# An elementwise product of a selective-scan stage, moved from VectorE to GpSimd

## Chip, core and metric

One core of one Trainium2 chip. The metric is the device time of one launch in microseconds. The traced execution is shown with it; its span runs from the first to the last instruction of the trace.

## What is computed

The kernel is one block: adaptive layer norm, a mamba layer, a residual, another adaptive layer norm, and a mixture of experts with a residual. Input x is 4 x 2048 x 256 in float32. The change touches the mamba layer alone, of which this matters:

```python
xs = silu(causal_conv(x @ in_proj_w[:512].T) + conv_b)       # b, l, 512
dt, B, C = split(xs @ x_proj_w.T, [64, 80])
delta = softplus(dt @ dt_proj_w.T + dt_proj_b)               # b, l, 512
A = -exp(A_log)                                              # 512, 16
h[t] = exp(delta[t] * A) * h[t-1] + (delta[t] * xs[t]) * B[t]  # 512 x 16 states
y[t] = sum over the 16 states of h[t] * C[t]
out = (y * silu(res)) @ out_proj_w.T
```

The factor `delta * xs` (one value for each channel and time step, shared by the 16 states) is the product that the change moves.

## The kernel before

Four programs run one behind the other: setup, mamba, the shared expert with the routing, and the routed experts. The mamba program goes through 16 chunks of 512 time steps, four to a sequence. Within a chunk there are 16 sets s = 0 to 15 of 32 channels each; a set has 32 channels x 16 states, held as 128 partitions x 4 groups x 512 steps in a ring of eight tiles `hs`. Bodies for chunks 0, 1, 14 and 15 are written out; chunks 2 to 13 run in a loop of four.

For each set the work goes round the engines:

- `states_in` (L620 on VectorE, L709 on GpSimd) multiplies u = delta * xs, replicated over the states, by B and writes `hs`. For ten sets ("own": 0, 1, 3, 4, 6, 8, 9, 11, 12, 14) VectorE does this from `u_ps`, which TensorE's `spread_u` (L427) fills by a matmul with a 0/1 matrix. For the six "shared" sets (2, 5, 7, 10, 13, 15) GpSimd does it from `u_rep`, which four DMAs of SP's queue (L335) fill. Both read `us[:, half]`, and both wait for `du_ready`.
- ScalarE makes `dA` = exp(delta * A) (L555), four of a set, three ahead of the scans at most.
- VectorE scans (`scan_set`, L641), four scans of 128x512 for a set. ScalarE saves the last column as the state (`save`, L560).
- GpSimd multiplies the scanned set by C (`weigh_states`, L724).
- TensorE sums over the states (`sum_states`, L437), four sets at a time, at steps s = 1, 5, 9, 13; it needs `weigh_states` of these four sets. Its result `y_ready` lets the ring tiles be filled again: `states_in` of sets 4, 8 and 12 on VectorE, and of each shared set on GpSimd, wait for it. VectorE gates y with silu(res) (`gate_y`, L654).

Besides, each engine prepares the next chunks at fixed steps of the present one. TensorE's order is the table `plan`: XS (input projection, L396), CV (convolution, L400), RS, XP (L404), DT and DB (L407), T (transposes of the normalized x, L391), OP (output projection, L415). They share two PSUM banks, so each waits for the eviction of the last but one. At s = 14 TensorE does, in this order, T 0, T 1 (for chunk c + 2) and `spread_u` of set 0 (chunk c + 1); at s = 15 XS 0, XS 1 (chunk c + 2) and `spread_u` of set 1. ScalarE evicts what `evict` names, runs `normalize` (L536) at s = 14, and silu, exp and log at the steps of L244. `delta` for the next chunk is finished by VectorE's `add_delta` (L617) after the scans of sets 11 and 12, and `weigh_u` (L648) then makes `us = delta * us` for all 512 channels in one instruction of 128x2048, after the scan of set 13. It releases `du_ready`.

GpSimd's order in a chunk: weigh_states s for s = 0 to 15, the product of set 5 after s = 1, 7 after 3, 10 after 5, 13 after 8, 15 after 10, and that of set 2 of the next chunk after 14. After s = 11 it runs `rsqrt` (L700 to L707), four small instructions on 128x4 for the layer norm of chunk c + 2.

SP's queue carries all transfers of this stage in order. At the end of a chunk: `spread_bc` (B and C of the next chunk), `spread_delta` of quarter 0 (d_rep, L326), `spread_u` of set 2 (L335), and then the next chunk's d_rep of quarter 1, u_rep of sets 5 and 7, and the residual's input. `hold` is a wait for a semaphore with an increment of another behind it.

Of the kernel before, what the change touches and what calls it, by code (L numbers as in the profile page):

```python
# [21 lines left out]
ALU = mybir.AluOpType  # L22
# [13 lines left out]
KI = DI // P  # L36
# [20 lines left out]
def hold(eng, sem, value, held):  # L57


    eng.wait_ge(sem, value)  # L60
    eng.sem_inc(held, 1)  # L61
# [132 lines left out]
def mamba_program(nc, ins, t, bc_dram, x1_dram, wout_dram):  # L194
# [4 lines left out]
    with ExitStack() as ctx:  # L199
# [7 lines left out]
        xpad, us, res = t["xpad"], sb("us", [P, 2, KI, T]), sb("res", [P, 2, KI, T])  # L207
        xdbl = sb("xdbl", [PROJ, T])
        delta, xres = sb("delta", [P, KI, T]), sb("xres", [P, TT, D])
# [10 lines left out]
        xdbl_made, dt_made, db_made, out_made = sem("xdbl_made"), sem("dt_made"), sem("db_made"), sem("out_made")  # L220
        halo_ready = sem("halo_ready")
        xs_ready, us_pre, us_ready, res_pre, res_ready = sem("xs_ready"), sem("us_pre"), sem("us_ready"), sem("res_pre"), sem("res_ready")
        xdbl_ready, bc_kept, bc_loaded = sem("xdbl_ready"), sem("bc_kept"), sem("bc_loaded")
        abs_ready, exp_ready, log_ready, delta_ready, du_ready = sem("abs_ready"), sem("exp_ready"), sem("log_ready"), sem("delta_ready"), sem("du_ready")
# [4 lines left out]
        held, wout_loaded = sem("held"), sem("wout_loaded")  # L229
# [11 lines left out]
                 10: [("RS", 3)], 15: [("T", 0), ("T", 1)]}  # L241
        SHARED_AT = {1: (5,), 3: (7,), 5: (10,), 8: (13,), 10: (15,), 14: (2,)}
        RESIDUAL_AT, DELTA_AT = {4: (0,), 5: (1,)}, {11: (0, 1), 12: (2, 3)}
        SUM_AT, SILU_AT, SILU_RES_AT, EXP_AT, LOG_AT, STATS_AT, RSTD_AT, DU_AT, NORM_AT, EARLY = 1, 5, 11, 9, 10, 11, 11, 13, 14, 14  # L244
        order = [g for s in range(NSET) for g in plan.get(s, [])]
        back = [g for g in order if g[0] == "OP"]
        early = [g for s in range(EARLY, NSET) for g in plan.get(s, []) if g not in back]
# [8 lines left out]
        has_front = lambda c: not (known(c) and c == NCHUNK - 1)  # L256
# [27 lines left out]
        def read_bank(eng, g, f):  # L284
            eng.wait_ge(made[g[0]], many[g[0]] * f + g[1] + 1)
            return banks[bank_of[g]]
# [311 lines left out]
        @block.vector  # L598
        def _(dve):
            def layernorm(f):  # L600
                dve.wait_ge(x_loaded, 16 * f + 16)
                for tt in range(TT):
                    last = nc.vector.bn_stats(stats[:, tt, :], xin[:, tt, :])
                last.then_inc(ln_step, 1)
                hold(dve, ln_step, f + 1, held)
                if not (known(f) and f == 0):
                    hold(dve, xn_ready, f, held)
                for tt in range(TT):
                    last = nc.vector.bn_aggr(mv[:, tt, :], stats[:, tt, :])
                last.then_inc(stats_ready, 1)  # L610

            def add_delta(f, j):

                ps_ = read_bank(dve, ("DB", j), f)
                if j == 0:
                    dve.wait_ge(log_ready, f + 1)
                nc.vector.scalar_tensor_tensor(out=delta[:, j, :], in0=ps_[:, :], scalar=0.0, in1=delta[:, j, :],  # L617
                                               op0=ALU.max, op1=ALU.add).then_inc(delta_ready, 1)

            def states_in(c, s, par):  # L620

                i = OWN_SETS.index(s)
                dve.wait_ge(u_made, N_OWN * c + i + 1)
                if s % KI == 0 and not (known(c) and c == 0 and s < RING):
                    dve.wait_ge(y_ready, SPC * c + (s - RING) // KI + 1)
                if s == 0:
                    dve.wait_ge(bc_loaded, 16 * 2 * NF * (c + 1))
                nc.vector.tensor_tensor(hs[:, s % RING], u_ps[:, i % 2, :].unsqueeze(1).to_broadcast([P, NG, T]),  # L628
                                        b_rep[:, par, :].rearrange("p (g t) -> p g t", g=NG), ALU.mult).then_inc(dbu_own, 1)

            def scan_set(c, s, m):
                if s in OWN_SETS:
                    dve.wait_ge(dbu_own, N_OWN * c + OWN_SETS.index(s) + 1)
                else:
                    dve.wait_ge(dbu_shared, N_SHARED * c + SHARED_SETS.index(s) + 1)
                if m:
                    dve.wait_ge(state_saved, NSET * (c - 1) + s + 1)
                for g in range(NG):
                    u = NG * s + g
                    dve.wait_ge(da_ready, NG * NSET * c + u + 1)  # L640
                    nc.vector.tensor_tensor_scan(hs[:, s % RING, g, :], dA[:, u % ABANK, :], hs[:, s % RING, g, :], state[:, u:u + 1] if m else 0.0,  # L641
                                                 ALU.mult, ALU.add).then_inc(scan_done, 1)

            def weigh_u(f, half):
                dve.wait_ge(delta_ready, KI * (f + 1))
                dve.wait_ge(us_ready, f + 1)
                dve.wait_ge(xdbl_made, f + 1)
                nc.vector.tensor_tensor(us[:, half], delta[:], us[:, half], ALU.mult).then_inc(du_ready, 1)  # L648

            def gate_y(c, j, half):  # L650
                dve.wait_ge(y_ready, KI * c + j + 1)
                if j == 0:
                    dve.wait_ge(res_ready, c + 1)
                nc.vector.tensor_tensor(res[:, half, j, :], y_ps[:], res[:, half, j, :], ALU.mult).then_inc(yg_ready, 1)  # L654

            def residual(c, j):

                ps_ = read_bank(dve, ("OP", j), c - 1)
                if j == 0:
                    dve.wait_ge(xres_loaded, 16 * c)  # L660
                nc.vector.tensor_tensor(xres[:, 2 * j:2 * j + 2, :], ps_[:].rearrange("p (h d) -> p h d", h=2), xres[:, 2 * j:2 * j + 2, :],
                                        ALU.add).then_inc(x1_ready, 1)

            def body(c, m):
                par = m % 2
                states_in(c, 0, par)
                for s in range(NSET):
                    if s + 1 in OWN_SETS and (s + 1) % KI:
                        states_in(c, s + 1, par)
                    scan_set(c, s, m)  # L670
                    if s + 1 in OWN_SETS and (s + 1) % KI == 0:
                        states_in(c, s + 1, par)
                    if has_ahead(c) and s == STATS_AT:
                        layernorm(c + 2)
                    if has_back(c) and s == 3:
                        gate_y(c - 1, SPC - 1, 1 - par)
                    if has_back(c):
                        for j in RESIDUAL_AT.get(s, ()):
                            residual(c, j)
                    if s > SPC and s % SPC == 3:  # L680
                        gate_y(c, s // SPC - 1, par)
                    if has_front(c):
                        for j in DELTA_AT.get(s, ()):
                            add_delta(c + 1, j)
                        if s == DU_AT:
                            weigh_u(c + 1, 1 - par)

            layernorm(0)
            for j in range(KI):
                add_delta(0, j)  # L690
            weigh_u(0, 0)
            layernorm(1)
            bodies(dve, body)
            gate_y(NCHUNK - 1, KI - 1, 1)
            residual(NCHUNK, 0)
            residual(NCHUNK, 1)

        @block.gpsimd
        def _(pool):
            def rsqrt(f):  # L700
                hold(pool, stats_ready, f + 1, held)
                nc.gpsimd.tensor_scalar(var[:], mv[:, :, 1], EPS, None, ALU.add).then_inc(rstd_step, 1)
                nc.gpsimd.tensor_scalar(mean[:], mv[:, :, 0], -1.0, None, ALU.mult).then_inc(rstd_step, 1)
                hold(pool, rstd_step, 3 * f + 2, held)
                nc.gpsimd.tensor_tensor(rstd[:], var[:], t["mhalf"][:, 0:TT], ALU.pow).then_inc(rstd_step, 1)
                hold(pool, rstd_step, 3 * f + 3, held)
                nc.gpsimd.tensor_tensor(shift[:], mean[:], rstd[:], ALU.mult).then_inc(shift_ready, 1)  # L707

            def states_in(c, s, par):  # L709

# [16 lines left out]
            def body(c, m):  # L727
                par = m % 2
                for s in range(NSET):
                    weigh_states(c, s, par)  # L730
                    for n in SHARED_AT.get(s, ()):
                        if n > s:
                            states_in(c, n, par)
                        elif has_front(c):
                            states_in(c + 1, n, 1 - par)
                    if s == RSTD_AT and has_ahead(c):
                        rsqrt(c + 2)

            rsqrt(0)
            rsqrt(1)  # L740
            for s in range(NSET):
                for n in SHARED_AT.get(s, ()):
# [611 lines left out]
```

## Time and profile before

| what | us |
|---|---|
| median of 3 runs | 3006.31 (3005.31 to 5768.12) |
| profiled execution | 3006.31 |
| its span | 3004.6 |

```profile
PE 2258.5 (75%) x7448; PEld 1050.1 (35%) x7449; DVE 2068.5 (69%) x2313; ACT 1320.5 (44%) x2151; POOL 1936.9 (64%) x800
PE   4678687688687787687787784349988930999998
DVE  3299999999999999999989999824444440222222
ACT  1465565565665665665665664302222200222221
POOL 0189889889989889889889889900000016455553
PEclk7778688687787787787787786679999975999999
```

PE is TensorE, DVE VectorE, ACT ScalarE, POOL GpSimd. The first line gives busy time, its share of the span and the number of instructions. The others cut the span in 40 slices of 75 us, with the busy share in tenths; PEclk is TensorE's granted clock in tenths of 2.4 GHz. The mamba stage is slices 3 to 26, where VectorE is at 9 and GpSimd at 8 or 9.

### The profile page before, as it was taken

How to read it: one execution, taken by the hardware profiler on the slowest of the kernel's cores; microseconds unless marked ns; L12 is line 12 of the kernel's file. 1: busy time of each engine (PE TensorE's matmuls, PEld its weight loads, DVE VectorE, ACT ScalarE, POOL GpSimd, SP SyncE). 2: the span in 40 equal slices, each digit the busy share in tenths (PEclk: the TensorE clock that was granted, in tenths of full speed). 3: DMA queues.
4: the chain of work that ended last, by engine and by line, in shares of the span. 5: the costliest groups of instructions: out<-in, count | busy, mean ns of one | idle time of the engine just before them, and what ended most of it. 6: DMA issues, size and time to landing. Idle time of an engine off the chain costs nothing. (4 is left out here: it accounts for less than half of the span.)

```text
span 3004.6 us, 29127 instructions
## 1 busy us (share of the span) xinstructions
PE 2258.5 (75%) x7448; PEld 1050.1 (35%) x7449; DVE 2068.5 (69%) x2313; ACT 1320.5 (44%) x2151; POOL 1936.9 (64%) x800
## 2 busy tenths in 40 slices
PE   4678687688687787687787784349988930999998
PEld 3223233233233233232232231135555520556654
DVE  3299999999999999999989999824444440222222
ACT  1465565565665665665665664302222200222221
POOL 0189889889989889889889889900000016455553
PEclk7778688687787787787787786679999975999999
DMA  3333433433433433424424342152111100222221
GB/s 110 75 75 74 99 82 74 99 84 78 102 75 72 102 79 80 102 65 90 94 75 93 90 94 63 35 217 63 63 50 55 63 23 7 84 84 85 86 85 51
DMA packets 113435, 238.40 MB, mean 79 GB/s; under 512 B 21516, under 2 KB 75534, under 8 KB 100752
## 3 DMA queue, kind: packets, MB, share of 16 engines
q1 hardware_dynamic: 93328, 189.86, 25.9%
q0 software_dynamic: 14368, 36.00, 4.1%
q10 hardware_dynamic: 5600, 11.01, 1.0%
q8 instruction: 48, 0.79, 0.1%
q14 instruction: 91, 0.75, 0.1%
HBM read 106.10 MB, written 39.20 MB: 48 GB/s over the span
## 5 line engine op out<-in xcount | busy, mean ns | idle before, releaser
L724 POOL TENSOR_TENSOR hs<-hs,c_rep 128x2048 f32<-128x2048 f32 x256 | 1158.3, 4540 | 80.0 <-ACT state L560 79.8
L555 ACT ACTIVATE dA<-d_rep,a 128x512 f32<-128x512 f32 x1024 | 683.6, 686 | 603.7 <-DVE hs L641 599.5
L641 DVE TENSOR_TENSOR_SCAN hs<-dA,state,hs 128x512 f32<-128x512 f32 x768 | 915.3, 1259 | 27.1 <-ACT dA L555 25.9
L717 POOL TENSOR_TENSOR hs<-u_rep,b_rep 128x2048 f32<-128x2048 f32 x96 | 433.4, 4514 | 106.0 <-PE y_ps L437 98.3
L396 PE MATMUL bank<-xin,w_in 128*128 128x512 f32 x512 | 333.2, 805 | 110.4 <-ACT xpad L491 86.3
L628 DVE TENSOR_TENSOR hs<-u_ps,b_rep 128x2048 f32<-128x2048 f32 x160 | 363.9, 2275 | 73.6 <-PE u_ps L427 72.8
L437 PE MATMUL y_ps<-hs,gather 128*32 128x512 f32 x2048 | 279.7, 695 | 134.1 <-POOL hs L724 134.1
L407 PE MATMUL bank<-xdbl,w_dt 65*128 65x512 f32 x256 | 181.3, 846 | 172.4 <-DVE delta L617 115.3
L641 DVE TENSOR_TENSOR_SCAN hs<-dA,hs 128x512 f32<-128x512 f32 x256 | 290.0, 1199 | 12.1 <-ACT dA L555 12.0
L822 POOL TENSOR_TENSOR rstd<-var,mhalf 128x4 f32<-128x4 f32 x16 | 16.1, 1006 | 409.4 <-DVE var L924 409.4
L1204 PE MATMUL z<-w1r,hT 128*128 x560 | 261.0, 609 | 2.6 <-issue 1.9
L1286 DVE TENSOR_TENSOR hid<-z,sg 128x512 f32<-128x512 f32 x70 | 48.4, 691 | 298.6 <-ACT sg L1264 298.6
L400 PE MATMUL bank<-xpad,w_conv 128*128 128x512 f32 x512 | 234.9, 607 | 4.1 <-ACT us L501 4.1
L396 PEld LDWEIGHTS bank<-xin,w_in 128*128 128x128 f32 x512 | 126.6, 258 | 305.9 <-issue 161.1
L427 PE MATMUL u_ps<-us,spread 32*128 32x512 f32 x320 | 212.7, 750 | 21.8 <-DVE hs L628 20.8
L437 PEld LDWEIGHTS y_ps<-hs,gather 128*32 128x32 f32 x2048 | 67.3, 126 | 359.9 <-issue 208.4
L1171 POOL DMA_INDIRECT out<-outr,cur x70 | 71.1, 1016 | 142.9 <-DVE outr L1279 142.6
L407 PEld LDWEIGHTS bank<-xdbl,w_dt 65*128 65x128 f32 x256 | 58.2, 252 | 270.2 <-DVE delta L617 136.5
L1204 PEld LDWEIGHTS z<-w1r,hT 128*128 128x128 f32 x560 | 101.6, 191 | 120.5 <-issue 120.4
L400 PEld LDWEIGHTS bank<-xpad,w_conv 128*128 128x128 f32 x512 | 94.1, 191 | 141.6 <-issue 124.5
L868 PE MATMUL y_ps<-w2s,hid 128*128 128x256 f32 x512 | 119.1, 386 | 20.5 <-DVE yg L975 18.1
L1222 PE MATMUL y_ps<-w2r,hidT 128*128 x560 | 132.4, 379 | 0.8 <-ACT hidT L1253 0.8
(169 smaller groups left out, 2640.3 us busy)
## 6 DMA issues: line engine op xcount, KB each, us to landing
d_rep<-delta SPq DMA_DIRECT2D x256, 256.0 KB, 4.3
u_rep<-us SPq DMA_DIRECT2D x384, 64.0 KB, 2.2
b_rep<-bc_rows SPq DMA_DIRECT2D x64, 256.0 KB, 4.5
c_rep<-bc_rows SPq DMA_DIRECT2D x64, 256.0 KB, 7.4
xin<-in_x SPq DMA_DIRECT2D x16, 512.0 KB, 3.7
xres<-in_x SPq DMA_DIRECT2D x16, 512.0 KB, 3.6
x<-xres SPq DMA_DIRECT2D x16, 512.0 KB, 4.5
x_sb<-x SPq DMA_DIRECT2D x16, 512.0 KB, 4.2
```

What stands on the lines that cost most here:

```text
L396: last = nc.tensor.matmul(ps_[:, :], t["w_in"][:, k, col:col + P], hT[:, k, :], start=(k == 0), stop=(k == KD - 1))
L400: last = nc.tensor.matmul(ps_[:, :], t["w_conv"][:, j, k, :], xpad[:, j, k:k + T], start=(k == 0), stop=(k == KCONV - 1))
L407: last = nc.tensor.matmul(ps_[:, :], t["w_dt"][:, j * P:(j + 1) * P], xdbl[0:DT_ROWS, :], start=True, stop=True)
L427: nc.tensor.matmul(u_ps[:, i % 2, :], t["spread"][DS * q:DS * q + DS].rearrange("p f d -> p (f d)"), us[DS * q:DS * q + DS, par, j, :], st ...
L437: last = nc.tensor.matmul(y_ps[DS * q:DS * q + DS, :], t["gather"][:], hs[:, (SPC * j + q) % RING, g, :], start=(g == 0), stop=(g == NG - ...
L555: nc.scalar.activation(dA[:, u % ABANK, :], d_rep[:, q % 2, j, :], ACT.Exp, scale=t["a"][:, u:u + 1]).then_inc(da_ready, 1)
L628: nc.vector.tensor_tensor(hs[:, s % RING], u_ps[:, i % 2, :].unsqueeze(1).to_broadcast([P, NG, T]), b_rep[:, par, :].rearrange("p (g t) -> ...
L641: nc.vector.tensor_tensor_scan(hs[:, s % RING, g, :], dA[:, u % ABANK, :], hs[:, s % RING, g, :], state[:, u:u + 1] if m else 0.0, ALU.mul ...
L717: nc.gpsimd.tensor_tensor(hs[:, s % RING], u_rep[:, i % UBUF, :].unsqueeze(1).to_broadcast([P, NG, T]), b_rep[:, par, :].rearrange("p (g t ...
L724: nc.gpsimd.tensor_tensor(hs[:, s % RING, :, :], hs[:, s % RING, :, :], c_rep[:, par, :].rearrange("p (g t) -> p g t", g=NG), ALU.mult).th ...
L1204: last = nc.tensor.matmul(z[:, q % 2, half, :], hT[:, q % 2, i, :], t["w1r"][:, e, i, half * H:(half + 1) * H], start=(i == 0), stop=(i == ...
L1222: last = nc.tensor.matmul(y_ps[:, :], hidT[:, q % 2, i, :], t["w2r"][:, e, i, :], start=(i == 0), stop=(i == KI - 1))
```

## The change

`weigh_u` moves from VectorE's program to GpSimd's, as the same product on the same tiles. On VectorE it stood after the scan of set 13 (DU_AT = 13). On GpSimd it stands after `weigh_states` of set 12 (DU_AT = 12), behind `rsqrt` of set 11. The first one, for chunk 0, stands between `rsqrt(0)` and `rsqrt(1)`. Its three waits stay; the one for `delta_ready` is now a `hold`, since another engine makes it.

```diff
-        SUM_AT, SILU_AT, SILU_RES_AT, EXP_AT, LOG_AT, STATS_AT, RSTD_AT, DU_AT, NORM_AT, EARLY = 1, 5, 11, 9, 10, 11, 11, 13, 14, 14
+        SUM_AT, SILU_AT, SILU_RES_AT, EXP_AT, LOG_AT, STATS_AT, RSTD_AT, DU_AT, NORM_AT, EARLY = 1, 5, 11, 9, 10, 11, 11, 12, 14, 14
@@ VectorE
-            def weigh_u(f, half):
-                dve.wait_ge(delta_ready, KI * (f + 1))
-                dve.wait_ge(us_ready, f + 1)
-                dve.wait_ge(xdbl_made, f + 1)
-                nc.vector.tensor_tensor(us[:, half], delta[:], us[:, half], ALU.mult).then_inc(du_ready, 1)
-
@@ VectorE, body
-                        if s == DU_AT:
-                            weigh_u(c + 1, 1 - par)
@@ VectorE, before the bodies
-            weigh_u(0, 0)
@@ GpSimd
+            def weigh_u(f, half):
+                hold(pool, delta_ready, KI * (f + 1), held)
+                pool.wait_ge(us_ready, f + 1)
+                pool.wait_ge(xdbl_made, f + 1)
+                nc.gpsimd.tensor_tensor(us[:, half], delta[:], us[:, half], ALU.mult).then_inc(du_ready, 1)
@@ GpSimd, body
+                    if s == DU_AT and has_front(c):
+                        weigh_u(c + 1, 1 - par)
 
             rsqrt(0)
+            weigh_u(0, 0)
             rsqrt(1)
```

## Rows read from the trace of the kernel before

**Rows 1.** Busy time by stretch: us, then busy and count for each engine, clock, DMA.
```profile
0.00:1968.00 1968.00, 1433.80 (x4496) 554.60 (x4497) 1738.57 (x1560) 1115.78 (x1795) 1636.68 (x432) 0.78 0.35 83
```

**Rows 2.** VectorE's groups, 200 to 1900 us: busy us, mean ns, idle before.
```profile
L641 DVE TENSOR_TENSOR_SCAN hs<-dA,state,hs 128x512 f32<-128x512 f32 x737 | 878.5, 1259 | 27.1 <-ACT dA L555 25.9
...
L648 DVE TENSOR_TENSOR us<-delta,us 128x2048 f32<-128x2048 f32 x15 | 38.0, 2533 | 0.0
```

**Rows 3.** GpSimd's largest group, 200 to 1900 us.
```profile
L724 POOL TENSOR_TENSOR hs<-hs,c_rep 128x2048 f32<-128x2048 f32 x241 | 1090.9, 4541 | 63.8 <-ACT state L560 63.6
```

**Rows 4.** Waits, 200 to 1900 us: who waited for whom, total, times, longest.
```profile
POOL 0189889889989889889889889900000016455553
...
DVE hs L628 <- PE u_ps L427: 55.7, 29, 3.6
```

**Rows 5.** GpSimd's timeline in chunk 7: start, duration, instruction, idle before.
```profile
1007.66 4.51 POOL L717 TENSOR_TENSOR hs<-u_rep,b_rep 128x2048 f32<-128x2048 f32 x1 [5.40 <-PE y_ps L437]
...
1032.08 2.34 POOL L707 TENSOR_TENSOR shift<-mean,rstd 128x4 f32<-128x4 f32 x1 [0.18 <-POOL rstd L705]
1034.38 13.48 POOL L724 TENSOR_TENSOR hs<-hs,c_rep 128x2048 f32<-128x2048 f32 x3
...
1057.88 4.51 POOL L724 TENSOR_TENSOR hs<-hs,c_rep 128x2048 f32<-128x2048 f32 x1 [1.09 <-ACT state L560]
```

**Rows 6.** VectorE's timeline in chunk 7 and at the start of chunk 8.
```profile
1032.10 2.26 DVE L648 TENSOR_TENSOR us<-delta,us 128x2048 f32<-128x2048 f32 x1
...
1044.28 2.28 DVE L628 TENSOR_TENSOR hs<-u_ps,b_rep 128x2048 f32<-128x2048 f32 x1
1050.08 2.29 DVE L628 TENSOR_TENSOR hs<-u_ps,b_rep 128x2048 f32<-128x2048 f32 x1 [3.52 <-PE u_ps L427]
```

**Rows 7.** TensorE's timeline there; each matmul leaves two records.
```profile
1030.11 5.84 PE L437 MATMUL y_ps<-hs,gather 128*32 128x512 f32 x32 [5.50 <-POOL hs L724]
1038.33 1.97 PE L391 MATMUL bank<-ident,xin 128*128 128x128 f32 x8 [2.37 <-ACT xin L536]
1040.23 2.07 PE L427 MATMUL u_ps<-us,spread 32*128 32x512 f32 x2
1042.40 6.60 PE L396 MATMUL bank<-xin,w_in 128*128 128x512 f32 x8
1048.92 1.12 PE L427 MATMUL u_ps<-us,spread 32*128 32x512 f32 x2
```

**Rows 8.** GpSimd's timeline in chunks 0 and 14, and its end of chunk 15.
```profile
211.72 4.52 POOL L717 TENSOR_TENSOR hs<-u_rep,b_rep 128x2048 f32<-128x2048 f32 x1 [6.14 <-PE y_ps L437]
...
238.28 0.20 POOL L707 TENSOR_TENSOR shift<-mean,rstd 128x4 f32<-128x4 f32 x1 [0.18 <-POOL rstd L705]
...
1803.35 4.51 POOL L717 TENSOR_TENSOR hs<-u_rep,b_rep 128x2048 f32<-128x2048 f32 x1 [5.06 <-PE y_ps L437]
...
1927.39 22.39 POOL L724 TENSOR_TENSOR hs<-hs,c_rep 128x2048 f32<-128x2048 f32 x5
```

**Rows 9.** VectorE's timeline, `weigh_u` in chunk 14.
```profile
1826.07 6.32 DVE L648 TENSOR_TENSOR us<-delta,us 128x2048 f32<-128x2048 f32 x1
```

**Rows 10.** TensorE's timeline, XS 0 and 1 in chunks 0 and 13.
```profile
244.73 5.37 PE L396 MATMUL bank<-xin,w_in 128*128 128x512 f32 x8 [1.88 <-ACT xin L488]
...
1724.74 5.06 PE L396 MATMUL bank<-xin,w_in 128*128 128x512 f32 x8
```

**Rows 11.** VectorE's timeline, the product of set 1 after chunks 0 and 13.
```profile
251.18 2.29 DVE L628 TENSOR_TENSOR hs<-u_ps,b_rep 128x2048 f32<-128x2048 f32 x1 [2.57 <-PE u_ps L427]
...
1730.89 2.29 DVE L628 TENSOR_TENSOR hs<-u_ps,b_rep 128x2048 f32<-128x2048 f32 x1 [1.99 <-PE u_ps L427]
```

**Rows 12.** The page's DMA issues: KB each, median us from issue to landing.
```profile
u_rep<-us SPq DMA_DIRECT2D x384, 64.0 KB, 2.2
```

**Rows 13.** TensorE's timeline in the prologue.
```profile
70.36 3.70 PE L396 MATMUL bank<-xin,w_in 128*128 128x512 f32 x8 [0.69 <-ACT xpad L491]
```

**Rows 14.** TensorE by stretch, chunk 7: us, busy (records), granted clock, DMA.
```profile
1042.00:1044.00 2.00, 1.90 (x3) 0.50 0.95 197
```

## The prediction

> **What bounds the kernel now.** I read the page's busy shares and slices first, then the busy time by stretch, then the groups of each engine, the waits, and at last the timelines of one chunk on three engines. The reader should see four things.
>
> First, the change lies wholly in the first 1968 us, the mamba stage, where VectorE is busy 1738.6 us and GpSimd 1636.7 us [rows 1]. Two engines are near full, so work taken from one lands on another that has little room.
>
> Second, VectorE's work there is mostly the scans at 1.26 us each; the instruction to be moved is one of 128x2048 per chunk, 38.0 us for 15 of them in that window [rows 2]. 15 of the 16 lasted 2.26 us, one 6.32. GpSimd's main instruction has the same form (two SBUF inputs, 128x2048, f32) and takes 4.54 us [rows 3]: this is the price on GpSimd.
>
> Third, neither engine is simply full. VectorE loses 55.7 us in 29 waits for u_ps from TensorE, GpSimd 98.3 us in 29 waits for y_ps [rows 4]. So each chunk is a loop through several engines, and the loop's path decides, not a sum of busy time.
>
> Fourth, where the loop runs. I take chunk 7 and three points. S is the start of GpSimd's `states_in` for set 13, which waited 5.40 us for TensorE: 1007.66. From S GpSimd works without a gap through weigh_states 9, 10, the product of set 15, weigh_states 11, the four small instructions of `rsqrt`, and weigh_states 12, which starts at 1034.38 [rows 5]. On VectorE `weigh_u` ran at 1032.10; the first product of the next chunk, set 0, began at 1044.28, and that of set 1 at 1050.08, after 3.52 us of waiting for TensorE [rows 6]; call this last point R. On TensorE the order is: sum_states, two transposes T, `spread_u` of set 0 (1040.23), XS 0 and 1 (1042.40), `spread_u` of set 1 (1048.92) [rows 7]. XS began as soon as ScalarE had evicted T, which lies behind VectorE's scan of set 15. So R minus S went through VectorE: 42.42 us in this chunk.
>
> **What the change does, step by step.**
>
> *Taken from VectorE.* One `weigh_u` a chunk, 2.26 us, 2.2 from its start to the next. All VectorE points behind it come 2.2 us earlier, if nothing else holds them.
>
> *Taken from GpSimd.* A gain that the diff does not name. `rsqrt`'s last instruction took 2.34 us in chunk 7 and ended just as `weigh_u` did [rows 5, 6]; in chunk 0 the same instruction took 0.20 us [rows 8], and the hold fell on another instruction. In each of chunks 0 to 13 one GpSimd instruction is 1.2 to 2.1 us too long while `weigh_u` runs. In chunk 14, where `rsqrt` is left out, `weigh_u` met a large GpSimd instruction and lasted 6.32 us, 4.06 more than usual [rows 9]. So the two engines shut each other out in this form. The other VectorE instructions there read at most one SBUF tensor beside PSUM and run over GpSimd's without such a trace. I take 2.1 us as the relief.
>
> The Trainium skill says the same ("SBUF — State Buffer", Who interferes with whom): a VectorE instruction with two SBUF inputs contends with a GpSimd one that reads SBUF, and the first to start holds the port throughout. By that rule the product on GpSimd, beside PSUM-fed VectorE work, stalls nobody; without the relief each chunk's end below would come 2.1 us later. The trace agrees with the rule: 0.20 against 2.34 us.
>
> *Added to GpSimd.* One `weigh_u`, 4.51 us, after weigh_states 12. Its end D, counted from S: weigh_states 12 starts at 26.72 (1034.38 - 1007.66), less 2.14 of relief = 24.58, plus 4.49 for it and 4.51 for the new product, D = S + 33.6. Its own waits cost nothing: `add_delta` 3 stands before `weigh_u` on VectorE today, which began at 1032.10 [rows 6], and the product on GpSimd starts at S + 29.1 = 1036.8. Today `us` is ready at 1034.3, S + 26.6. So it is ready 7 us later, though VectorE is 2.2 us earlier.
>
> *Who is queued behind.* TensorE waits in order: `spread_u` of set 0 needs `du_ready`, and XS 0, XS 1 and `spread_u` of set 1 stand behind it. Today XS starts at S + 34.02 on average (14 chunks, first 33.01, last 34.51 [rows 8, 10]). After, `spread_u` of set 0 starts at D + 0.1 = S + 33.7. It takes 1.12 us in 10 of the 14 chunks and 2.07 in 4, mean 1.39; XS 0 and 1 take 5.06 to 6.69, mean 5.74 (14 rows, first 5.37, last 5.06 [rows 10]); `spread_u` of set 1 takes 1.12 [rows 7]. With overlaps of 0.07 at the two joins: 33.7 + 1.32 + 5.67 + 1.16 to VectorE's start = S + 41.9. Today R is at S + 40.85 on average (14 chunks; first 251.18 - 211.72 = 39.46 [rows 8, 11]). So R comes 1.0 us later: 14 x 1.0 = +14 us. The 2.2 us of VectorE are gone, as a longer wait for u_ps.
>
> *From R to the next S.* 72.8 us in the mean, and I take it as unchanged, since it is made by VectorE, ScalarE and TensorE in turns. The 14 differences lie close together (last 1803.35 - 1730.89 = 72.5 [rows 8, 11]; longest 73.5). For that GpSimd must not be late at the next set 13. It starts the next chunk's weigh_states 0 at D + 18 = S + 51.6, where today it is at S + 50.2 [rows 5]. It is 1 to 3 us late, and then has its 1.09 us of waits for ScalarE and the 5.40 at set 13 to catch up [rows 5]. The sum agrees: 22 large instructions at 4.48, `rsqrt` 2.2 and the product 4.5 make 105.3 us, against a period of 113.7 (1803.35 - 211.72 over 14 [rows 8]).
>
> *SP's queue.* The u_rep transfers of set 2 wait for `du_ready` too, and the next d_rep behind them. Between D and its use GpSimd has weigh_states 13 and 14, 9 us; from issue to landing such a transfer takes 2.2 us [rows 12], and four are issued in 2.4: hidden. Without that work between, it would cost about 4.6 us.
>
> *Chunk 14 and the end.* Nothing is transposed there, and VectorE wins 6.2 us. But in the second half of the last chunk GpSimd runs without a pause: weigh_states 11 to 15 go in one piece and end at 1949.8 (1927.39 + 22.39 [rows 8]), with TensorE's last sum behind them. Up to there its queue also got 4.5 us more. I give 2 us of the 6 as gain. The prologue's product is 2.3 us longer once; XS of chunk 1 stands before `spread_u` there, so I count zero (cover gone: +2.3).
>
> **Sum.** 14 x 1.0 - 2 = +12 us. The profiled execution is itself the median run, 3006.3 (span 3004.6). Forecast 3018.7 us.
>
> **Bounds of the unknown term.** It is TensorE's pace over twelve matmul records right behind a wait. All fast: XS in 3.70 as in the prologue [rows 13], R at S + 39.5, 1.3 earlier: 14 x -1.3 - 2 = -20, 2986 us. All at the lower level, as in chunk 7 (granted clock 0.50 of 2.4 GHz, so 1.2 [rows 14]): 2.07, 6.60 and 2.07 give S + 44.3, 3.5 later: +47, 3053 us. I take the mean of the 14 because the clock there falls and rises within most chunks. A wait of 3 to 4 us in front pushes to the slow side, so I keep it near the middle, not below.
>
> **Rivals.**
> 1. *VectorE's gain survives.* If `us` is early enough on GpSimd, or TensorE's order does not pin XS, each chunk wins 2.2 us: 14 x -2.2 - 2 = -33, 2973 us. For it: VectorE is the busiest engine. Against: D is at S + 33.6, and twelve records do not fit between it and S + 38.6, even at the fast pace (5.8 us).
> 2. *Slower, by TensorE's clock.* TensorE now stands idle from the end of T to S + 33.7; T ended at S + 32.6 in chunk 7 (1038.33 + 1.97 [rows 7]) and comes up to 2.2 us earlier with VectorE. If the clock is then low for all that follows, and also in the stretch from R to S (73.5 us in the slowest chunk against 72.8), each chunk loses 3.5 + 0.7: 14 x 4.2 - 2 = +57, 3063 us. It decides if more than about ten of the twelve records run at 1.2 GHz. For it: chunk 7 is such a one. Against: 9 of the 14 XS pairs took under 5.5 us.
> 3. *GpSimd itself becomes the bound.* Needs 113.7 us of work, has 105.3: it would need 8 us more a chunk. Only then would time rise by more than 2%.
> 4. *Nothing moves*: later u_ps exactly eats the early VectorE, 3006 us within 5. It is inside the forecast's own range.
>
> **Chances.** Forecast mechanism (GpSimd's product sets XS), 2986 to 3045: 0.72, rival 4 in it. Rival 1: 0.14. Rival 2: 0.10. Rival 3: 0.02; others 0.02. For 8 in 10 the range runs from 2975, the end of rival 1, to 3050. By more than 2% (60 us, about what a measurement here can tell from no change) faster: 0.02, since even rival 1 gives 1.1%. Slower by more than 2%: half of rival 2 and rival 3, 0.07. Within 2%: 0.91.
>
> **What would show it.** No VectorE instruction of 128x2048 from two SBUF tensors; 16 of 4.5 us on GpSimd; `rsqrt`'s four never longer than 1.04. VectorE's waits for u_ps grow from 55.7 to over 85 us, those of GpSimd for y_ps shrink from 98 to about 60. TensorE waits for GpSimd's `us` 3 us in each chunk, before `spread_u` of set 0. XS starts at S + 35. It would be wrong if R minus S fell below 40, if GpSimd stopped waiting at set 13, or if R to S changed by more than 1 us.

## The result

| | median us | runs |
|---|---|---|
| before | 3003.34 | 20 |
| changed | 3036.19 | 20 |

The ratio is 1.0104, 95% interval 1.0091 to 1.0117: the change costs 1.04%, some 33 us. The traces say 3035.2 against 3004.6 us of span. Among the 20 executions of the kernel before, one took 5768 us and one 3036; the median isn't moved by them.

The table compares the two traces by the points that the prediction used (S: GpSimd's product of set 13; R: VectorE's product of set 1; means over chunks 0 to 13, worked out from the timelines).

| us from S | before | forecast | changed |
|---|---|---|---|
| product on GpSimd ends (D) | - | 33.6 | 33.6 |
| `spread_u` of set 0 starts | 31.3 | 33.7 | 33.7 |
| its duration | 1.39 | 1.39 | 1.96 |
| XS 0 and 1, duration | 5.74 | 5.74 | 6.04 |
| R | 40.85 | 41.9 | 42.76 |
| from R to the next S | 72.84 | 72.8 | 73.10 |

The waits, 200 to 1900 us: first the engine and line that waited, then who was waited for, the total, the times and the longest. The first line of [rows 4] is one of the page's slices and no wait; the wait of the kernel before that the prediction reads as 98.3 us is this one:

```profile
POOL hs L717 <- PE y_ps L437: 98.3, 29, 6.3
```

The changed kernel:

```profile
DVE hs L628 <- PE u_ps L427: 115.8, 46, 4.9
...
POOL hs L714 <- PE y_ps L437: 96.4, 29, 6.1
...
PE u_ps L427 <- POOL us L704: 62.0, 15, 4.3
```

VectorE's wait for u_ps doubled, from 55.7 us, and TensorE has a new wait of 62.0 us in 15 times for GpSimd's `us`. That is the queue that the prediction described. Chunk 7 on GpSimd, the answer to [rows 5]:

```profile
1020.83 4.51 POOL L714 TENSOR_TENSOR hs<-u_rep,b_rep 128x2048 f32<-128x2048 f32 x1 [5.34 <-PE y_ps L437]
...
1045.23 0.20 POOL L698 TENSOR_TENSOR shift<-mean,rstd 128x4 f32<-128x4 f32 x1 [0.18 <-POOL rstd L696]
1045.42 4.55 POOL L721 TENSOR_TENSOR hs<-hs,c_rep 128x2048 f32<-128x2048 f32 x1
1049.94 4.50 POOL L704 TENSOR_TENSOR us<-delta,us 128x2048 f32<-128x2048 f32 x1
```

The product ends at 1054.44, S + 33.61. The last instruction of `rsqrt` takes 0.20 us, where it took 2.34. TensorE and VectorE in the same chunk, to be held against [rows 7] and [rows 6]:

```profile
1043.26 5.80 PE L437 MATMUL y_ps<-hs,gather 128*32 128x512 f32 x32 [5.63 <-POOL hs L721]
1049.15 1.09 PE L391 MATMUL bank<-ident,xin 128*128 128x128 f32 x8
1054.57 2.07 PE L427 MATMUL u_ps<-us,spread 32*128 32x512 f32 x2 [4.33 <-POOL us L704]
1056.56 6.05 PE L396 MATMUL bank<-xin,w_in 128*128 128x512 f32 x8
1062.54 1.12 PE L427 MATMUL u_ps<-us,spread 32*128 32x512 f32 x2
```

```profile
1040.40 14.20 DVE L641 TENSOR_TENSOR_SCAN hs<-dA,state,hs 128x512 f32<-128x512 f32 x12
1054.51 0.67 DVE L648 TENSOR_TENSOR res<-y_ps,res 128x512 f32<-128x512 f32 x1
1056.85 2.29 DVE L628 TENSOR_TENSOR hs<-u_ps,b_rep 128x2048 f32<-128x2048 f32 x1 [1.67 <-PE u_ps L427]
1063.70 2.29 DVE L628 TENSOR_TENSOR hs<-u_ps,b_rep 128x2048 f32<-128x2048 f32 x1 [4.56 <-PE u_ps L427]
```

VectorE runs its twelve scans of sets 13 to 15 without the product in between and then waits twice, 1.67 and 4.56 us, for TensorE. TensorE stands idle for 4.33 us after the transposes, and the two records of `spread_u` behind that wait take 2.07 us, XS 6.05.

### The profile page after: what moved, and what is told of

The parts are those of the page before. It is cut to its first block and busy times, and to the rows that moved or that the text cites. A ratio compares the mean times of both kernels' runs of the same rounds, so it can differ in the third digit from the quotient of the medians.

```text
span 3035.2 us, 29143 instructions
## 1 busy us (share of the span) xinstructions
PE 2270.4 (75%) x7448; PEld 1053.1 (35%) x7449; DVE 2030.8 (67%) x2297; ACT 1321.1 (44%) x2151; POOL 1980.8 (65%) x816
## 5 line engine op out<-in xcount | busy, mean ns | idle before, releaser
L396 PE MATMUL bank<-xin,w_in 128*128 128x512 f32 x512 | 342.9, 826 | 91.2 <-ACT xpad L491 86.3
L427 PE MATMUL u_ps<-us,spread 32*128 32x512 f32 x320 | 222.2, 782 | 72.8 <-POOL us L704 62.0
L1286 DVE TENSOR_TENSOR hid<-z,sg 128x512 f32<-128x512 f32 x70 | 48.4, 692 | 298.4 <-ACT sg L1264 298.4
```

What stands on the lines that cost most here:

```text
L396: last = nc.tensor.matmul(ps_[:, :], t["w_in"][:, k, col:col + P], hT[:, k, :], start=(k == 0), stop=(k == KD - 1))
L427: nc.tensor.matmul(u_ps[:, i % 2, :], t["spread"][DS * q:DS * q + DS].rearrange("p f d -> p (f d)"), us[DS * q:DS * q + DS, par, j, :], st ...
```

## The experiments

Three theories were held against each other. **Queue**: time is lost because `us` comes late to TensorE, with XS and the second `spread_u` behind it. **Load**: the 4.5 us more on GpSimd (or what VectorE does) set the pace. **Clock**: a large part is TensorE's pace behind the idle time. All times are medians, and the ratios are against the kernel before, which took 3005 to 3006 us beside each of these runs. Where a run is compared with the changed kernel, that is the 3036.19 us above. "XS" stands for XS 0 and 1 together, eight records.

### The product one place earlier on GpSimd

```diff
- ... RSTD_AT, DU_AT, NORM_AT, EARLY = ... 11, 12, 14, 14
+ ... RSTD_AT, DU_AT, NORM_AT, EARLY = ... 11, 11, 14, 14
```

> The changed kernel with the product on GpSimd one place earlier, after rsqrt of set 11 and before weigh_states 12. Queue theory (the time is lost because `us` reaches TensorE's queue late, with XS 0 and 1 behind it): the product ends at S + 29.1 instead of S + 33.6, before TensorE's transposes end, so XS again starts right behind ScalarE's eviction of T, 2.2 us earlier than in the kernel before; S to R falls from 42.8 to about 38.7 us, and the time to about 3036 - 14 x 4.1 = 2979 us, under that of the kernel before by some 25. Load theory (GpSimd with 4.5 us more a chunk is what costs): nothing changes, 3036 us.

Measured: 2962.9 us, ratio 0.986 (0.9845 to 0.9878). The profiled execution took 2949.8, two of the six runs being near 2950 and four near 2963. The product ends at S + 29.2, and TensorE waits at most 0.26 us for it. Chunk 7, S = 977.55:

```profile
1006.24 1.09 PE L391 MATMUL bank<-ident,xin 128*128 128x128 f32 x8
1007.27 1.12 PE L427 MATMUL u_ps<-us,spread 32*128 32x512 f32 x2
1009.04 3.70 PE L396 MATMUL bank<-xin,w_in 128*128 128x512 f32 x8 [0.65 <-ACT xin L488]
```

The load theory falls: GpSimd has the same work and the time is 73 us less. The median went 16 us below the expected 2979. The trace is of one of the two faster executions, 29 us below it. In this trace XS took 3.67 to 3.70 us in 8 of the 14 chunks and 5.40 in six, which makes the mean S to R 37.4 us against the expected 38.7, 18 us in all. R to S is 0.5 us shorter than in the changed kernel, another 8 us. There is no trace of an execution near 2963, so what sets the two groups apart isn't shown; their granted clock over the whole execution was 0.832 against 0.840. The move to GpSimd as such is good; the place in the order made it bad.

In the eight faster chunks TensorE had stood idle for 0.64 to 1.05 us before XS, in the six others for 1.85 to 1.93, as here in chunk 5:

```profile
783.18 1.12 PE L427 MATMUL u_ps<-us,spread 32*128 32x512 f32 x2
786.23 5.40 PE L396 MATMUL bank<-xin,w_in 128*128 128x512 f32 x8 [1.93 <-ACT xin L488]
```

### XS 0 ahead of `spread_u` on TensorE

```diff
                         if is_there(g, c):
                             group(g, c, chunk_of(g, c), par)
+                        if g == ("XS", 0) and has_front(c):
+                            spread_u(c + 1, 0, 1 - par)
...
-                    if s + 2 >= NSET and has_front(c):
+                    if s + 2 > NSET and has_front(c):
```

> The changed kernel with TensorE's `spread_u` of set 0 moved behind XS 0 (before XS 1); GpSimd as in the changed kernel. Queue theory: XS 0 starts at S + 32 (T evicted), `spread_u` 0 at about S + 35, XS 1 ends at S + 39; S to R about 40 instead of 42.8, TensorE's waits for `us` nearly gone, time about 3036 - 14 x 2.8 = 2997 us. Load theory: 3036 us.

Measured: 2978.0 us, ratio 0.991 (0.9892 to 0.9925). GpSimd is untouched, the product still ends at S + 33.6, and 58 us are gone. Chunk 7, S = 996.20:

```profile
1027.71 1.98 PE L396 MATMUL bank<-xin,w_in 128*128 128x512 f32 x4 [1.70 <-ACT xin L490]
1029.96 1.12 PE L427 MATMUL u_ps<-us,spread 32*128 32x512 f32 x2 [0.26 <-POOL us L706]
1031.00 1.98 PE L396 MATMUL bank<-xin,w_in 128*128 128x512 f32 x4
```

XS 0 fills the wait, which is down to 0.26 us here. VectorE's product of set 0 starts no earlier than before (S + 36.2 in the mean, 35.9 in the changed kernel), and R comes at S + 39.2 instead of 42.8. So it was what stood behind the late `us` that counted, not the lateness of set 0 itself. Again the gain is larger than expected (58 against 39 us), and again the matmuls are at the fast pace here: 1.98 us for an XS group. The swap closes the idle time too, so this run holds queue and clock together and does not share the 58 us out between them; the next one holds the order fixed.

### Matmuls into the idle time

```diff
-                if i == 0:
-                    pe.wait_ge(du_ready, c + 1)
                 if not (known(c) and c == 0 and i < 2):
                     pe.wait_ge(dbu_own, N_OWN * c + i - 1)
+                if i == 0:
+                    if not (known(c) and c == 0):
+                        for _ in range(4):
+                            nc.tensor.matmul(u_ps[:, 0, :], t["ident"][:], t["w_in"][:, 0, 0:T], start=True, stop=True)
+                    pe.wait_ge(du_ready, c + 1)
```

> The changed kernel with four added 128x512 matmuls on TensorE between T 1 and the wait for `us` (their result is overwritten by `spread_u`). They fill the 4.3 us in which TensorE is idle, if they run at the higher clock (3.4 us). Clock theory (0.9 of the 1.9 us of later R come from TensorE being at 1.2 GHz after that idle time): `spread_u` 0 takes 1.1 instead of 2.07 us and XS below 5.5 instead of 6.05, S to R falls by 1.5 us or more, time about 3015 us. If the clock doesn't depend on it, no change or, where the four run at 1.2 GHz (6.8 us), a later XS: 3036 to 3080 us.

Measured: 2987.8 us, ratio 0.994 (0.9926 to 0.9959). TensorE does more, in the same place of the same order, and the kernel is 48 us faster than the changed one, and faster than the kernel before. Chunk 7, S = 994.55:

```profile
1023.84 3.60 PE L428 MATMUL u_ps<-w_in,ident 128*128 128x512 f32 x8
1028.23 1.12 PE L430 MATMUL u_ps<-us,spread 32*128 32x512 f32 x2 [0.79 <-POOL us L707]
1029.28 3.70 PE L396 MATMUL bank<-xin,w_in 128*128 128x512 f32 x8
1032.91 1.12 PE L430 MATMUL u_ps<-us,spread 32*128 32x512 f32 x2
```

The twelve records behind the wait take 5.8 us instead of 9.1. The granted clock over these stretches, first of this kernel (1.00, 2.4 GHz throughout), then of the changed one (0.63, a mix of both levels); columns are those of [rows 14]:

```profile
1028.20:1034.00 5.80, 5.77 (x12) 1.00 0.52 113
```

```profile
1054.50:1063.70 9.20, 9.10 (x12) 0.63 0.68 144
```

S to R is 39.5 us in each chunk, which is the fast bound of the prediction (S + 39.5). The changed kernel has 42.76 in the mean: 3.25 us a chunk, 14 x 3.25 = 45.5 us, and 48.4 were measured.

### Two instead of four

```diff
-                        for _ in range(4):
+                        for _ in range(2):
```

> The changed kernel with two added matmuls in front of the wait for `us` instead of four (four gave 2988 us). They cover 1.7 of the 4.3 us of TensorE's idle time. Clock theory, if what counts is how long TensorE stands idle in front of XS: part of the gain, some chunks with XS at 3.7 us and some with 5.4 to 6, 3000 to 3025 us. If the four only helped by something else than the idle time they fill (their place, or the wait that moved in front of them), two give the same 2988 us.

Measured: 3033.6 us, ratio 1.0095 (1.0078 to 1.0112). Below the expected gain: 13 of 14 chunks kept XS at 5.06 to 6.43 us, and one, chunk 1, had 3.70. Chunk 7:

```profile
1045.80 1.88 PE L428 MATMUL u_ps<-w_in,ident 128*128 128x512 f32 x4
1050.23 2.07 PE L430 MATMUL u_ps<-us,spread 32*128 32x512 f32 x2 [2.55 <-POOL us L707]
1052.23 6.08 PE L396 MATMUL bank<-xin,w_in 128*128 128x512 f32 x8
```

With 2.55 us of idle time left instead of 4.33, nearly all the cost is still there; with 0.79 us left none is. The added matmuls as such, or the wait that moved in front of them, are not what helped. The cost goes by steps, not in proportion to the idle time. Chunk 1, the one at the fast pace, had 2.10 us of idle time left, the others 2.28 to 2.57.

### Other work on VectorE

```diff
+                        if s == 13:
+                            for i in range(6):
+                                nc.vector.bn_stats(pad[:, i, :], t["w_in"][:, 0, 0:D])
```

> The changed kernel with about 2.1 us of other work on VectorE after the scan of set 13, where `weigh_u` stood (six bn_stats of 128x256 of a weight, into an unused tile). Queue theory: VectorE waits 1.7 + 4.6 us for u_ps a chunk in the changed kernel, so this is hidden: 3036 us within 4, and the waits of VectorE for u_ps fall by about 2 us a chunk. If VectorE's load bounds the chunk: +2.1 x 15 = 3067 us.

Measured: 3036.8 us, ratio 1.0104 (1.0088 to 1.0121), as the changed kernel. In chunk 7:

```profile
1045.06 2.04 DVE L681 BATCH_NORM_STATS2 pad<-w_in 128x6 f32<-128x256 f32 x6
...
1057.00 2.28 DVE L628 TENSOR_TENSOR hs<-u_ps,b_rep 128x2048 f32<-128x2048 f32 x1
1063.65 2.29 DVE L628 TENSOR_TENSOR hs<-u_ps,b_rep 128x2048 f32<-128x2048 f32 x1 [4.37 <-PE u_ps L427]
```

The 2.04 us vanish in the wait before set 0, which was 1.67 us, and a little of the next. What the change took from VectorE is therefore worth nothing in the changed kernel. On TensorE the transposes come about 2 us later in ten of the 14 chunks, behind ScalarE's normalize, and so part of its idle time lies in front of them. In chunk 7 that leaves 2.39 us in front of `spread_u` instead of 4.33, and XS took 6.03 us all the same.

### The product one place later on GpSimd

```diff
- ... RSTD_AT, DU_AT, NORM_AT, EARLY = ... 11, 12, 14, 14
+ ... RSTD_AT, DU_AT, NORM_AT, EARLY = ... 11, 13, 14, 14
```

> The changed kernel with the product on GpSimd one place later, behind weigh_states 13. Queue theory: it ends at S + 38.1, everything behind it in TensorE's queue moves by the full 4.5 us, S to R is 47.3 us: 3036 + 14 x 4.5 = 3099 us. Load theory (only GpSimd's work counts, not its place): 3036 us.

Measured: 3087.5 us, ratio 1.0277 (1.026 to 1.0294): 51 us more than the changed kernel, not 63. The product ends at S + 38.1 as worked out, S to R is 46.8 us in the mean, 4.1 more instead of 4.5, since XS took 5.5 instead of 6.04 us, and R to S shrank by 0.4. So lateness is paid almost in full from S + 33.6 to S + 38.1, and this time not through the clock, which moves the price by some tenths the other way. TensorE in chunk 7:

```profile
1085.75 2.06 PE L427 MATMUL u_ps<-us,spread 32*128 32x512 f32 x2 [8.65 <-POOL us L704]
1087.74 5.45 PE L396 MATMUL bank<-xin,w_in 128*128 128x512 f32 x8
```

Behind 8.65 us of idle time XS was 0.6 us faster than behind 4.33: more idle time in front is not always a slower pace. Why is open.

### `weigh_u` on VectorE, one set earlier

The kernel before, with its DU_AT at 12 instead of 13.

> The kernel before with `weigh_u` still on VectorE but one set earlier, behind add_delta 3 (set 12). `us` is ready some 14 us before TensorE asks for it, and XS waits for T as it did. Queue theory: no gain from the earlier `us`, 3005 us within 8. Port theory (the two engines shut each other out for these products): it now meets one of GpSimd's large instructions in each chunk, so that one such instruction a chunk lasts about 6.6 instead of 4.5 us, or `weigh_u` lasts longer than 2.26 us. Without exclusion both keep 4.5 and 2.26.

Measured: 2991.5 us, ratio 0.9955 (0.9938 to 0.9972). That is 14 us under the 3005.6 beside it, which was not expected. GpSimd and VectorE in chunk 7:

```profile
1019.06 6.58 POOL L724 TENSOR_TENSOR hs<-hs,c_rep 128x2048 f32<-128x2048 f32 x1
```

```profile
1018.99 2.29 DVE L648 TENSOR_TENSOR us<-delta,us 128x2048 f32<-128x2048 f32 x1
```

VectorE's product started first and weigh_states 11 lasted 6.58 instead of 4.5 us. This is the exclusion seen in [rows 9] and [rows 5], here with GpSimd's large instruction as the one held. Over the run `weigh_u` took 2.29 to 4.35 us. sum_states starts about 2 us later therefore, XS starts at S + 34.9 instead of 34.0, and yet S to R is 39.8 instead of 40.85 us, since XS took 3.7 us in 13 of 14 chunks:

```profile
1036.21 3.70 PE L396 MATMUL bank<-xin,w_in 128*128 128x512 f32 x8 [1.92 <-ACT xin L488]
```

Behind the same 1.92 us XS took 5.40 to 6.66 us in four chunks of the kernel before, as in chunk 6:

```profile
926.84 6.35 PE L396 MATMUL bank<-xin,w_in 128*128 128x512 f32 x8 [1.92 <-ACT xin L488]
```

So the idle time right in front of XS does not by itself decide its pace. Here the transposes follow sum_states without idle time (at most 0.2 us, but for chunk 0); in the kernel before TensorE stood idle for 0.4 to 2.7 us in front of them. That the clock is higher because the work behind sum_states lies closer together is my reading; this run does not separate it.

### Two matmuls behind `spread_u`

```diff
+                if i == 0 and not (known(c) and c == 0):
+                    pe.wait_ge(dbu_own, N_OWN * c)
+                    for _ in range(2):
+                        nc.tensor.matmul(u_ps[:, 1, :], t["ident"][:], t["w_in"][:, 0, 0:T], start=True, stop=True)
```

In the kernel before:

> The kernel before with two added 128x512 matmuls on TensorE behind `spread_u` of set 0 (into the half of u_ps that set 1 overwrites), where it stood idle for 1.8 to 2 us before XS 0. Clock theory: XS at 2.4 GHz, 3.7 instead of 5.6 us, S to R 39 instead of 40.85 us, 3003 - 14 x 1.8 = 2978 us; a little less if the two delay XS. Otherwise 3003 us or up to 20 more.

Measured: 2984.3 us (2977 to 3000), ratio 0.9939 (0.9915 to 0.9964). XS took 3.7 us in 11 of the 14 chunks and 3.83 to 4.07 in the rest. So the kernel before, too, was paying for the clock, 21 us against the 3005.6 beside it. In chunk 7 of this run `weigh_u` started 0.13 us behind a large product of GpSimd and took 6.54 us:

```profile
1017.26 11.05 POOL L728 TENSOR_TENSOR hs<-hs,c_rep 128x2048 f32<-128x2048 f32 x2
```

```profile
1017.39 6.54 DVE L652 TENSOR_TENSOR us<-delta,us 128x2048 f32<-128x2048 f32 x1
```

S to R was 47.9 us there against 37.6 to 41.2 in the others. In the kernel before, `weigh_u` met GpSimd's small instructions in 13 of the chunks 0 to 13 (in chunk 6 it started just ahead of weigh_states 12, which then took 6.62 us), and this one shows what it can cost when GpSimd's large one starts first.

With the product on GpSimd before weigh_states 12, and the same two matmuls:

> The product on GpSimd before weigh_states 12 (as in the first experiment of this study, 2963 us) with the same two added matmuls behind `spread_u` of set 0. 6 of its 14 chunks had XS at 5.40 us, the rest at 3.70; clock theory: all at 3.7, worth 6 x 1.7 = 10 us; the two added ones take 1.7 us where the gap is 1.0 to 2.0, so XS starts up to 0.7 us later in eight chunks: 2950 to 2962 us. If it is nothing: 2963 us or more.

Measured: 2954.0 us, ratio 0.983 (0.9814 to 0.9847). XS took 3.6 to 3.7 us in all 14 chunks. This is the lowest median of the study, 52 us under the 3005.6 beside it. TensorE in chunk 7:

```profile
1011.76 1.98 PE L432 MATMUL u_ps<-w_in,ident 128*128 128x512 f32 x4
1013.58 3.60 PE L396 MATMUL bank<-xin,w_in 128*128 128x512 f32 x8
```

The expectation took "six chunks at 5.40 us" from the trace of the 2950 us execution and the 2963 us from the median, which do not belong together. Trace against trace, S to R is 37.4 us in both kernels: what XS gains, its later start takes back. The four executions here (2952.7 to 2956.5) lie below the 2963 group of the first experiment and above its two at 2950. So the two matmuls lowered the median by 9 us, and that they did it through XS in the slower group is likely but not shown, since no trace of that group exists.

### Three more in front of sum_states

```diff
+                    if s == 13:
+                        pe.wait_ge(dbu_own, N_OWN * (c + 1) - 1)
+                        for _ in range(3):
+                            nc.tensor.matmul(u_ps[:, 0, :], t["ident"][:], t["w_in"][:, 0, 0:T], start=True, stop=True)
```

> The product before weigh_states 12, the two added matmuls behind `spread_u` of set 0 (2954 us), and three more in front of sum_states at step 13, where TensorE stands idle for 6.8 us and sum_states then takes 6.4 instead of 3.6 us. Clock theory: sum_states at up to 2.4 GHz, T 1 to 2.7 us earlier. What stands behind T is held by ScalarE's normalize and its eviction after the scans of set 15, so little of it comes through: 2945 to 2955 us. If the three run long at 1.2 GHz and hold up sum_states, 2960 us.

Measured: 2968.0 us, ratio 0.9875 (0.9859 to 0.9892), 14 us slower than without them. sum_states of chunk 7 did go at the fast pace, 3.64 us, but S to R and R to S grew by 0.3 and 0.5 us in the mean. The 0.3 us are the two matmuls behind `spread_u`. In seven of the 14 chunks they took 3.2 to 3.7 us instead of 1.98, and R came at about S + 38.5, in the others at S + 36.8. Chunk 2:

```profile
463.25 3.68 PE L432 MATMUL u_ps<-w_in,ident 128*128 128x512 f32 x4
466.76 3.60 PE L396 MATMUL bank<-xin,w_in 128*128 128x512 f32 x8
```

So the filling can itself run at the slow pace and then holds up what stands behind it. Where the 0.5 us from R to S come from is open.

## Why the prediction was right in its mechanism and wrong in its size

**What bounds the kernel: right.** A loop through GpSimd, TensorE and VectorE with S and R on it. Moving the product by one place changed the time by -73 and +51 us, with the engines' instructions unchanged.

**The price on GpSimd and the relief: right.** 4.50 us and D = S + 33.61, with 33.6 forecast. The 0.20 us of `rsqrt`'s last instruction in all chunks, against 0.20 to 2.42 before, bear out that VectorE's product used to hold GpSimd's. (Over the 14 chunks the hold was 1.1 to 2.2 us, 1.8 in the mean. The sum used chunk 7's own 2.14 with chunk 7's own start, so D is not hurt by it.) The Trainium skill's rule ("SBUF — State Buffer", Who interferes with whom) agrees with the trace here: 6.58 us for a GpSimd product when VectorE's two-input one starts first, 6.54 for VectorE's when GpSimd's does.

**Who is queued behind: right.** TensorE waits 4.1 us a chunk for `us` (3 forecast; the transposes end earlier, at S + 29.5 instead of 31.3, as their waits for normalize fell from 22.1 us in all to 1.6). VectorE's 2.2 us are gone.

**The step that failed is the term for TensorE's pace over the twelve records behind the wait.** The prediction gave it the mean of the 14 chunks before, 1.39 and 5.74 us, and named a longer wait's push to the slow side without pricing it. Measured: 1.96 and 6.04 us, 0.87 us more a chunk, 14 x 0.87 = 12 us. The sum has a second and smaller miss, R to the next S, 0.26 us longer, 3.7 us. And the gain at the end was 1.0 us of time to the stage's end (164.7 from S of chunk 14 before, 163.8 after) instead of 2. With the forecast's 12 this makes 29 us; 1.7 of the 30.6 us between the spans lie behind the mamba stage (1038.2 against 1036.5 us), which the change does not touch.

The mean of before was the wrong price because TensorE's idle time lies elsewhere. Before, `spread_u` followed the transposes at once and XS came behind 0.1 to 2.0 us of waiting; now all twelve records stand behind 4.2 us (3.8 to 4.3). The experiments with four and two matmuls show that in the changed kernel filling this time frees the twelve from the low clock, and filling less than half of it does not. They do not give a rule by which the pace could have been foretold: in other kernels of this study XS took 3.7 us in one and 5.4 to 6.7 us in another behind the same 1.92 us, and was faster behind 8.65 than behind 4.33. What else decides is open.

All twelve at 2.4 GHz give S + 39.5 and a kernel of 2988 us, so the clock over these records is worth 48 us in the changed kernel, more than the change's loss of 33. Without it, the change with its queue would have beaten the kernel before as that one ran, though not that kernel with its own XS at the fast pace (2984 us).

**Rivals.** Rival 1 (VectorE's gain survives) was wrong for this change, but its condition, `us` early enough, was met one place earlier, and the kernel then took 2963 us, 10 less than the 2973 of that rival; the surplus is not the rival's doing, since in the trace XS ran at the fast pace in 8 chunks and R came at S + 37.4, where the rival had S + 38.6. Rival 2 (the clock) was the missing part: seven or eight of the twelve records ran slow in chunk 7 (two of `spread_u`, and (6.05 - 3.70) / 0.43 = 5.5 of XS), short of the ten to twelve it wanted, and the time came to lie between forecast and rival. Rival 3 fell: GpSimd still waits 5.5 us at set 13 (5.6 before).

**The sign that was wrong.** GpSimd's waits for y_ps were to shrink from 98 to about 60 us and stayed at 96. The 38 us less are the new 4.5 us less the relief, some 2.4 a chunk, at an unchanged period. But the prediction itself had the chunk 1.0 us longer, and it became 2.2 us longer (115.9 against 113.7), which gives GpSimd nearly all of it back.

## What to carry to other kernels

An instruction that releases another engine is to be placed by when it ends in that engine's queue and what stands behind it, before its load is counted: the same move cost 1% at one place and gained 1.4% one place earlier. When an idle gap on TensorE changes, the records behind it must be priced for that gap, from rows at each level of the clock, not by the mean of all. If a gap cannot be closed, a few matmuls without a use, or real work brought forward into it, can be worth a try: four of them gained 3.3 us a chunk in a gap of 4.3. It has to be tried for each gap: two gained nearly nothing there, and three more in another gap cost 14 us.

## What the runs showed of the hardware

- TensorE's granted clock behind 4.3 us of idle time was 0.63 over the next twelve records, behind 0.8 us it was 1.00, and with 2.3 to 2.6 us idle XS was still slow in 13 chunks.
- The length of the idle time did not decide alone: behind 1.92 us the same eight records took 3.70 us in one kernel and 5.40 to 6.66 in another, and behind 8.65 us they took 5.45, less than the 6.05 behind 4.33.
- On GpSimd and VectorE, products with two SBUF inputs of 128x2048 shut each other out to the end of the one that started first: 2.1 us were lost where GpSimd's was held (6.58 instead of 4.5), 4.3 us where VectorE's was (6.54 instead of 2.26). VectorE's scans, with one input in PSUM, kept their 1.26 us, and GpSimd's product its 4.5 us beside them and beside bn_stats.
- More work on TensorE (14 chunks x 4 matmuls) made a kernel 48 us faster.
